# The last group's closing two octets later, group 6's residual first, the last residual in three pieces

## The reference, cut to what matters

```python
def reference(x, ...):
    x = x + _L0_cond_ref(x, ...)   # causal moving averages, gates, Wout, then a layer norm
    x = x + _L1_cond_ref(x, ...)   # attention: 16 heads of 8 channels, sparse or dense by row
    return x

# of _L1_cond_ref, per row of the batch:
    scores = jnp.einsum('bhqd,bhkd->bhqk', Q, K) * scale
    dense_out = jnp.einsum('bhqk,bhkd->bhqd', jax.nn.softmax(scores + bias, axis=-1), V)
```

## Time and profile before

| | value |
|---|---|
| time, median of three runs | 322.58 us (322.51, 322.58, 323.9) |
| the profiled execution's own time | 324.2 us |
| its span, first to last instruction | 322.4 us |
| PE busy | 300.0 us, 93% |
| DVE busy | 255.9 us, 79% |
| POOL busy | 247.5 us, 77% |
| ACT busy | 203.2 us, 63% |
| granted clock of PE, mean of the span | 0.989 |

### The profile page before, as it was taken

How to read it: one execution, slowest core, us unless ns; L and a number is a source line. 1 busy time by engine, 2 the same in 40 slices (tenths; PEclk the granted TensorE clock), 3 DMA queues, 4 the chain that set the end, 5 groups by cost and what they waited for, 6 DMA issues and landing times. The chain is left out here.

```text
span 322.4 us, 9923 instructions
## 1 busy us (share of the span) xinstructions
PE 300.0 (93%) x3326; PEld 200.0 (62%) x3326; DVE 255.9 (79%) x1422; ACT 203.2 (63%) x442; POOL 247.5 (77%) x300
## 2 busy tenths in 40 slices
PE   7897899999999999997886989999999999999995
PEld 2463546546374655635464668778788787787773
DVE  2488788687787876777768569999999999999972
ACT  5732247354554636467464687887877887877873
POOL 3174766795986876584737669999999999999990
PEclk9999999999999999999799899999999999999999
DMA  6700020231505033125301435644443354110011
GB/s 188 221 2 34 1 69 33 67 83 34 113 2 143 5 73 75 34 45 84 72 0 33 92 90 92 134 107 124 103 124 101 92 127 103 52 35 4 2 36 35
DMA packets 29154, 23.07 MB, mean 72 GB/s; under 512 B 2736, under 2 KB 27824, under 8 KB 29104
## 3 DMA queue, kind: packets, MB, share of 16 engines
q1 hardware_dynamic: 29104, 22.44, 28.9%
HBM read 7.75 MB, written 2.10 MB: 31 GB/s over the span
## 5 line engine op out<-in xcount | busy, mean ns | idle before, releaser
L1571 POOL TENSOR_TENSOR arena<-arena,neg_max 128x512 f32<-128x512 f32 x128 | 129.5, 1039 | 13.8 <-DVE neg_max L1415 13.6
L1415 DVE CUSTOM_DVE_ANT_0 arena<-ps,arena 128x128 f32<-128x128 f32 x512 | 113.6, 287 | 10.1 <-issue 5.0
L1080 ACT ACTIVATE arena<-ps 128x512 f32<-128x512 f32 x128 | 69.7, 596 | 10.5 <-PE ps L799 10.5
L799 PE MATMUL ps<-ident_sb,arena 128*128 128x128 f32 x512 | 69.0, 278 | 0.0
L799 PEld LDWEIGHTS ps<-ident_sb,arena 128*128 128x128 f32 x512 | 57.2, 142 | 6.9 <-POOL arena L1571 4.4
L1492 POOL TENSOR_TENSOR arena<-arena 128x448 f32<-128x448 f32 (+6 forms) x56 | 42.5, 759 | 14.1 <-DVE arena L1249 8.3
L1415 DVE DVE_READ_ACCUMULATOR2_ANT neg_max<- 128x1 f32 x512 | 42.6, 83 | 0.1
L815 PE MATMUL ps<-arena 128*32 128x128 f32 x1024 | 41.2, 279 | 0.0
L1479 POOL TENSOR_TENSOR arena<-decay_a,arena 128x192 f32<-128x192 f32 x32 | 17.9, 591 | 22.0 <-ACT arena L928 22.0
L815 PEld LDWEIGHTS ps<-arena 128*32 128x32 f32 x1024 | 24.1, 109 | 6.9 <-issue 0.3
L785 PE MATMUL ps<-arena 48*128 48x128 bf16 x512 | 25.6, 220 | 2.4 <-DVE neg_max L1415 2.4
(11 more groups left out here) (157 smaller groups left out, 516.8 us busy)
## 6 DMA issues: line engine op xcount, KB each, us to landing
arena<-q_parts SPq DMA_DIRECT2D x96, 64.0 KB
arena<-k_parts SPq DMA_DIRECT2D x96, 64.0 KB
arena<-in_x SPq DMA_DIRECT2D x16, 256.0 KB, 3.3
arena<-in_xt SPq DMA_DIRECT2D x8, 256.0 KB, 2.9
out<-arena SPq DMA_DIRECT2D x7, 256.0 KB, 3.1
arena<-in_consts SPq DMA_DIRECT2D x1, 420.0 KB, 3.7
w_sb<-in_w SPq DMA_DIRECT2D x1, 384.0 KB, 5.1
w_sb<-in_w SPq DMA_DIRECT2D x1, 192.0 KB, 3.9
```

What stands on the lines that cost most here:

```text
L799: mm = pe.transpose(ps[1][:, q % 2, k * P:k * P + P], neg_t[q % NT_RING][:, k * P:k * P + P], ident)
L1080: act.activation(probT[q % PT_RING], ps[1][:, q % 2, :], ACT.Exp, scale=-1.0)\
L1415: dve.tensor_tensor_reduce(out=neg_t[q % NT_RING][:, cs], in0=ps[0][:, score_bank(c) + slot, cs], in1=nbias[n % 2], scale=1.0, scalar=3.0e ...
L1571: pool.tensor_tensor(t4, t4, neg_max[:, n % 2, 4 * z:4 * z + 4].unsqueeze(2).broadcast_to([P, 4, P]), ALU.subtract).then_inc(s["shifted"], 1)
```

## The change

The diff is cut to the parts that move something; renumbered or empty lines are left out.

```diff
-SOLO = 10
+SOLO = 12
-        neg_t = [take(W) for _ in range(NT_RING - 2)] + xn
+        neg_t = [take(W) for _ in range(NT_RING - 2)]
+        neg_t[NT_RING - 3:NT_RING - 3] = xn
...
# PE, end()
                 b_locals(LAST, 1)
+                c_qk(LAST, 0)
                 scores(1)
-                c_qk(LAST, 0)
...
                 turn(1)
+                scores(3)
                 b_out(LAST, 1)
-                scores(3)
...
# PE, octet_step(c)
-                if c == 2:
-                    c_x1T(LAST, 1)
...
                 if 1 <= c and c + 3 < 2 * B:
                     scores(c + 3)
+                if c == 4:
+                    c_x1T(LAST, 1)
+                if c == 5:
+                    c_qk(LAST, 1)
+                if c == 6:
+                    c_less_both(LAST, 1, 0)
+                if c == 7:
+                    c_less_both(LAST, 1, 1)
+                if c == 8:
+                    c_v(LAST, 1)
...
# DVE, end()
                 logits(4)
+                logits(5)
                 b_mixed(LAST, 1)
-                logits(5)
-                c_moments(LAST, 1)
                 logits(6)
                 logits(7)
+                c_moments(LAST, 1)
                 c_centre(LAST, 1)
...
# DVE, octet_step(c)
-                if c == 1:
-                    c_residual(LAST, 1)
                 if 1 <= c and c + 3 < 2 * B:
                     logits(2 * c + 6)
                     logits(2 * c + 7)
+                if c in (1, 2):
+                    c_residual(LAST, 1, c - 1, c)
+                if c == 3:
+                    c_residual(LAST, 1, 2, GB)
...
# POOL
-                if c == 0:
-                    bias_sum(2)
...
-                if c == 1:
+                if c == 3:
                     c_keep(LAST, 1)
...
             def end():
+                c_residual(LAST, 0)
                 bias_sum(0)
-                c_residual(LAST, 0)
                 bias_sum(1)
...
                 shift(5)
+                bias_sum(2)
                 c_rstd(LAST, 1)
```

More of the change, by code:

```diff
@@ L1022, in step @@
                     f_hidden(i, m + 2)
-                c_part(i, m - 1, 0, 1)
-                c_values(i, m - 1)
                 if i * 2 + m == COUNTED:
@@ L1028, in step @@
                     act.activation(lncnt[:], cnt1[:], ACT.Ln).then_inc(s["lncnt_ready"], 1)
+                c_part(i, m - 1, 0, 1)
+                c_values(i, m - 1)
                 c_part(i, m - 1, 0, 2)
@@ L1104, in octet_step @@
                     c_values(LAST, 0)
-                if c == 2:
+                if c == 4:
                     c_x1T(LAST, 1)
-                if c in (3, 4, 5):
-                    c_parts(LAST, 1, c - 3)
-                if c == 6:
+                if c in (5, 6, 7):
+                    c_parts(LAST, 1, c - 5)
+                if c == 8:
                     c_values(LAST, 1)
@@ L1308, in c_centre, with c_residual @@
                                              ALU.subtract, ALU.mult).then_inc(s["centred"], 1)
-            def c_residual(i, m):
+            def c_residual(i, m, first, last):
                 u = m % 2
[L1313 to L1316, removed]
+                if first == 0:
+                    dve.wait_ge(s["rstd_ready"], grp(i, m, 1, 1))
+                    dve.wait_ge(s[f"xb_loaded{u}"], i * 16 + 16 * (m // 2 + 1))
+                    dve.wait_ge(s["centred"], grp(i, m, GB, GB))
                     dve.wait_ge(s["x1b_ready"], grp(i, m, 1, -1))
-                for b in range(GB):
+                for b in range(first, last):
                     cs = slice(b * P, b * P + P)
@@ L1322, in c_residual @@
                                                    ALU.mult, ALU.add)
-                ins.then_inc(s["x1_ready"], 1)
+                if last == GB:
+                    ins.then_inc(s["x1_ready"], 1)
             def front(i, m):
@@ L1401, in logits @@
                 if q == NT_RING - 3:
+                    dve.wait_ge(s["ctx_ps"], G)
+                if q == NT_RING - 1:
                     dve.wait_ge(s["mixed_ready"], G)
-                if q == NT_RING - 2:
-                    dve.wait_ge(s["ctx_ps"], G)
                 if q >= NT_RING:
@@ L1430, in result @@
                 dve.wait_ge(s["y_ps"], n + 1)
-                if n == 0:
-                    dve.wait_ge(s["x1b_ready"], G)
                 g, b = n // GB, n % GB
                 if b == 0:
+                    dve.wait_ge(s["x1b_ready"], g + 1)
                     dve.wait_ge(s[f"y_stored{g % 2}"], 16 * (g // 2 + 1))
```

## The result

The changed kernel takes 321.38 us, the median of seven runs (319.82 to 321.63); the kernel before, beside it, 323.9 (322.51 to 324.32, seven runs). The ratio is 0.9929 with a 95% interval of 0.9904 to 0.9955: 0.7% faster. Forecast were 318.7 us and a range of 316.5 to 321.3, so it was faster as expected, and the time lies just above the range.

What follows compares the result with a forecast made beforehand. POOL was taken as the bound, busy 59.97 of 60.00 us. Its earlier idleness was to fall from 15.95 to 11.1 us, 4.9 less: 324.2 to 319.3 profiled, a median of 318.7, range 316.5 to 321.3.

Steps and rivals of the forecast that it cites:

- the ledger: POOL's idleness before its full stretch: 15.95 us before, each microsecond removed ending the program a microsecond earlier.
- the sum: POOL's idleness after the change: 10.4 us, 11.1 with the pieces, for 15.95; 4.9 us less, profiled execution 319.3.
- the closing: Last group's closing, two octets later: POOL idles 4.5 us (1.1, 0.6, 1.6, 1.2) for 5.39; between 3.0 and 7.6.
- the pieces: Last group's residual on DVE in pieces, out of octet 1: 1.86 us wait to 0; sum with pieces 11.1 for 10.4.
- the head: POOL ahead of octet 1: idle 0.7 us for 1.84, 1.3 for 1.99, and 3.9 for 4.87.
- loads: SP's stack 2 loads would end at 192.6, scores(16) come near 200: hidden, with 5 us to spare.
- no granted clock of 0.5 after 150 us: Sign that the forecast holds: PE never drops to the 1.2 GHz level after 150 us.
- a fall in octets 4 to 8: Sign that the prediction is wrong: PE's clock falls in octets 4 to 8.
- the clock falls all the same: Rival: PE waits 1.3 us for quads 8 and 9, both half-clock stretches return, about 2 us: 320.7; chance 0.16.
- DVE held at the port: Rival: the residual's pieces cost the full 2.8 us, 2.1 more than forecast: 320.8 us; chance 0.08.
- the two rivals that rested on single banks: Two more octets on one bank pair: 321.1 us, no change (0.14 shared with nothing moves), or slower, 326.3 (0.07).
- what the median would be: Median put between 319.3 and 317.7 us, nearer the first: 318.7; chance 0.55.

Runs made afterwards that it cites:

- warm: Changed kernel with eight matmuls more, whose result nobody reads, on PE in octet 4 ahead of the turn of x1: 319.78 us.
- psum_input: Changed kernel with the last group's residual on DVE reading a PSUM bank in place of the centred SBUF tensor (values not the layer norm's): 318.4 us.
- before_warm: Kernel before with sixteen unused matmuls more in PE's waits (nine, three and four) around the turns of x1: 320.98 us.
- four_early: Changed kernel with the residual in four single operations in octets 1 and 2, the closing at octets 3 to 7 and SOLO 10: 319.91 us.
- front_only: Changed kernel with the closing put back at octets 2 to 6 ahead of the scores, residual whole in octet 1, SOLO 10: 320.87 us.
- whole_residual: Changed kernel with the last group's residual in one piece ahead of octet 1's logits, the closing still at octets 4 to 8: 322.25 us.
- one_input: Changed kernel with the last group's residual on DVE as a product alone, the addition of x left out: 321.0 us.

## Why the prediction was right, and where it was wrong

**Right: the ledger.** In fifteen of seventeen profiles, the two kernels' own among them, the span less POOL's idle time is 305.9 to 306.7 us. Of the sum's 11.1 the part before 171 us had 5.9 and measured 5.45; the closing with the pieces had 5.2 and measured 7.4, in warm 6.0. **Right: the head.** The turn of x1 was forecast at 152.4, shifts 0, 2, 4, 5 and 6 at 153.6, 158.2, 161.7, 162.7 and 167.6; they came at 152.2, 153.8, 157.9, 161.2, directly behind that, and 167.2. PE's wait before L429 is 0.26 (forecast under 0.3), the wait before rstd 1.98 (2.0), and eight shifts follow without idleness. Octet 3's turns came at 169.8 for 170.3. **Right: loads.** Stack 2's transfers end at 193.0, for 192.6.

**Wrong: "no granted clock of 0.5 after 150 us".** This is the step that failed. The sum holds only without a stretch: 4.9 us less than 322.4 is a span of 317.5, and the changed kernel has 318.0 where no stretch comes. With one it has 319.5, and by their clocks five of the seven runs beside the forecast and eight of the later twelve have one. It is also the prediction's own sign of being wrong, a fall in octets 4 to 8. The rival "the clock falls all the same" named the right mechanism with the wrong cause (PE's wait for quads 8 and 9, which was 1.14 and 0.20 us) and the wrong price: both stretches at 2 us together, where one costs 1.5.

**Mis-sized: the pieces.** 0.7 was taken for them, of a range to 2.8. Their operations last 3.24 us (0.62 + 0.35 + 2.27), four undisturbed ones 4 x 0.34 = 1.36, and psum_input, which takes only this away, has a span 318.0 - 316.3 = 1.7 us below the changed kernel without a stretch. The mechanism was the one named. What I had missed is where it lands (the rival "DVE held at the port" had up to 2.8 us for it and no clock): the last piece has two operations, both wait, and I had counted DVE as "ahead there" when PE needed both x1 and the next quads from it. The stretch is its consequence, so in a run with a stretch the pieces cost 1.7 + 1.5 = 3.2 us.

**Right in size, once x1 is in time: the closing.** 4.5 was forecast. Without the late x1, in psum_input, POOL idles 1.11 + 0.77 + 1.41 + 1.31 = 4.6, near the forecast's 1.1, 0.6, 1.6 and 1.2 one by one; in the changed kernel 7.2. What I had not seen is that it was not a gain to compare with 5.39: at full clock the early closing costs 0.82 + 1.03 + 1.50 + 0.49 = 3.8 in before_warm, and 1.5 of the 5.39 was the stretch. The page "Perfetto Trace Analysis" of the Trainium skill, section "Optimizing Tensor Performance", has independent matmul groups rotate through PSUM banks, which would make two more octets on one pair a loss. Of that four_early shows 0.2 us of idleness at most, and the two rivals that rested on single banks did not come: the first one's 321.1 us is near the 321.38 measured by coincidence, since without a stretch the changed kernel's span lies 1.5 us lower. Why the late closing idles POOL for 4.6 to 5.0 us where the early one takes 3.8 stays open: its place behind the scores was not tried alone.

**Wrong: what the median would be.** The scatter of before (322.5 or 323.9) was read rightly as one stretch more or less; the forecast of 318.7 then took credit for both stretches and for 0.6 more by the median. The measured gain hangs on the same count: it is 2.5 us against the first median of before, 323.9, where four of seven runs have two stretches, and 322.76 - 321.3 = 1.5 in the next batch.

## What to carry to other kernels

When the clock of the matmul engine falls in some stretch, time the kernel first with matmuls whose result nobody reads in the waits ahead of it: here that gave 320.98 us for the kernel before, which is the baseline that an edit has to beat at full clock. If a chain of short DVE operations with all inputs in SBUF lies beside a full POOL, cost each at up to the length of POOL's instruction and not its own; break the chain so that each stands alone behind other work, or read one input from PSUM. Work that stands in a wait also breaks it up: front_only and whole_residual differ in the place of the closing and what goes with it, and with the closing gone from octet 2 PE's waits of 2.26 and 1.03 us became one of 3.95, and the stretch 6.0 us for 3.4.

## What the hardware showed unexpectedly

- By these rows DVE and POOL take turns by whole instructions when DVE's tensors all lie in SBUF. A DVE operation of 0.34 us took up to 1.23 us beside shifts of 1.02 us, with two SBUF inputs, and up to 1.08 as a `tensor_scalar` with one; with one input from PSUM 0.35. Where DVE began first it lasted 0.35 and two shifts 2.19 for 2.04.
- A wait of PE as short as 1.35 us (one_input) or 1.79 (the changed kernel) was followed by some 3.4 us at 1.2 GHz, in some runs and not in others: by their mean clocks, four of ten runs of one_input and eight of twelve of the changed kernel had it. From 172 to 176 us, ahead of that fall, PE was busy for 2.02 us in the changed kernel. Eight unused matmuls in the wait removed the stretch, by the clock in all six runs.
- Each such stretch costs 1.3 to 1.6 us here, though PE is not the bound: at half clock the turns take 1.97 us in place of 1.04 to 1.09, and POOL waits for what stands behind them.
